# Groups of four tiles, DMA-transposed first states for all prepared tiles, and finishing work spread over two units in a five-layer graph network with GRU updates

## The reference

```
h = max(layernorm(x), 0)                          # (64, 128, 128)
A = (adj != 0)
for l in range(5):
    m   = h @ weight[l]
    agg = einsum('bij,bid->bjd', A, m)
    gi, gh = agg @ w_ih.T + b_ih, h @ w_hh.T + b_hh    # each split in r, z, n
    r, z = sigmoid(i_r + h_r), sigmoid(i_z + h_z)
    n = tanh(i_n + r * h_n)
    h = (1 - z) * n + z * h
out = x + h * nodemask[..., None]
```

## Time and profile before

| | |
|---|---|
| median of 3 runs | 381.57 us |
| the profiled execution's own time | 382.65 us |
| its span, first to last instruction | 380.9 us |
| busy: TensorE, VectorE, ScalarE, GpSimd | 96%, 82%, 78%, 73% |
| mean granted TensorE clock | 0.990 |
| share of time of the 16 DMA engines in the main queue | 52.4% |

### The profile page before, as it was taken

The page is one execution under the profiler, slowest core; times in us unless marked ns, Lnnn a source line. Parts: engine busy times, 40 slices in busy tenths (PEclk is TensorE's granted clock), DMA queues, the critical chain, the costliest instruction groups (busy, mean ns, idle before and its releaser), DMA issues.

```text
span 380.9 us, 6557 instructions
## 1 busy us (share of the span) xinstructions
PE 366.4 (96%) x2160; PEld 185.5 (49%) x2160; DVE 313.4 (82%) x574; ACT 297.1 (78%) x490; POOL 277.8 (73%) x261
## 2 busy tenths in 40 slices
PE   7769999999999999999999999999999999999992
PEld 3335555555555545445454545544455555555541
DVE  4794889888877879998989989887977778777785
ACT  3975889989878889798888978778767777677663
POOL 3555797797797889968685876757876655555796
PEclk9998999999999999999999999999999999999997
DMA  7836256387453844745285593407833432296422
GB/s 221 215 35 138 53 115 139 59 190 146 115 156 83 167 91 105 151 100 112 55 157 121 104 190 96 110 18 159 160 81 83 96 73 55 55 222 176 102 83 83
DMA packets 114128, 44.46 MB, mean 117 GB/s; under 512 B 91168, under 2 KB 107808, under 8 KB 114096
## 3 DMA queue, kind: packets, MB, share of 16 engines
q1 hardware_dynamic: 113856, 43.73, 52.4%
q10 hardware_dynamic: 144, 0.26, 0.2%
q0 software_dynamic: 96, 0.07, 0.1%
HBM read 17.57 MB, written 4.19 MB: 57 GB/s over the span
## 4 chain that ended last, share of the span: by engine, by line
PE 84%; DVE 7%; DMA 3%; POOL 2%; ACT 2%; issue 1%; SPq 0%; DVEq 0%; POOLq 0%; ACTq 0%
PE ps_r L270 9%; PE ps_r L271 8%; PE ps_z L270 8%; PE ps_r L272 8%; PE ps_z L271 8%; PE ps_z L272 8%; PE ps_s L341 4%; PE ps_s L340 4%; PE ps_in L272 4%; PE ps_in L271 4%; PE ps_in L270 4%; PE ps_hn L272 4%; PE ps_hn L270 4%; PE ps_hn L271 4%; DMA fold_in<-in_fold_lhs 1%
## 5 line engine op out<-in xcount | busy, mean ns | idle before, releaser
L747 POOL TENSOR_TENSOR zh<-z,h 128x512 f32<-128x512 f32 x80 | 101.6, 1270 | 81.3 <-ACT z L452 81.0
L446 ACT ACTIVATE r<-ps_r,b_sum,unscale 128x512 f32<-128x512 f32 x80 | 62.2, 778 | 51.1 <-PE ps_r L272 50.4
L577 DVE SCALAR_TENSOR_TENSOR rhn<-ps_hn,b_hn,r 128x512 f32<-128x512 f32 x80 | 60.0, 750 | 19.7 <-ACT r L446 19.4
L456 ACT ACTIVATE ps_in<-ps_in,b_ih,unscale 128x512 f32<-128x512 f32 x80 | 60.0, 750 | 19.0 <-DVE ps_in L583 17.2
L752 POOL TENSOR_TENSOR hp<-h,hp 128x512 f16<-128x512 f32 x64 | 74.4, 1162 | 0.0
L583 DVE TENSOR_TENSOR ps_in<-ps_in,rhn 128x512 f32<-128x512 f32 x80 | 56.0, 700 | 16.7 <-PE ps_in L272 14.6
L589 DVE SCALAR_TENSOR_TENSOR ps_in<-z,ps_in 128x512 f32<-128x512 f32 x79 | 54.6, 691 | 11.0 <-ACT ps_in L456 11.0
L452 ACT ACTIVATE z<-ps_z,b_sum,unscale 128x512 f32<-128x512 f32 x80 | 61.6, 770 | 1.0 <-PE ps_z L272 1.0
L594 DVE TENSOR_TENSOR h<-zh,ps_in 128x512 f32<-128x512 f32 x78 | 53.6, 688 | 9.7 <-POOL zh L747 1.9
L571 DVE TENSOR_TENSOR s_lo<-ps_s,s_hi 128x512 f16<-128x512 f32 x80 | 54.4, 681 | 0.0
L440 ACT CAST s_hi<-ps_s 128x512 f16<-128x512 f32 x80 | 46.6, 583 | 0.7
(11 more groups left out here) (109 smaller groups left out, 751.6 us busy)
## 6 DMA issues: line engine op xcount, KB each, us to landing
x_in<-in_x SPq DMA_DIRECT2D x16, 256.0 KB, 4.5
adj_in<-in_adj SPq DMA_DIRECT2D x16, 256.0 KB, 4.3
x_out<-in_xT SPq DMA_DIRECT2D x16, 256.0 KB, 3.0
mask_in<-in_mask_row SPq DMA_DIRECT2D x16, 256.0 KB, 3.7
out<-x_out SPq DMA_DIRECT2D x15, 256.0 KB, 2.3
nat<-hp SPq DMA_TRANSPOSE x64, 3.1
fold_in<-in_fold_lhs SPq DMA_DIRECT2D x1, 320.0 KB, 5.5
out<-x_out ACTq DMA_DIRECT2D x1, 256.0 KB, 2.6
```

The lines of the kernel that those rows point to most:

```text
L446: nc.scalar.activation(r[:], ps_r[:], ACT.Sigmoid, bias=b_sum[:, 0:1], scale=unscale[:, 0:1]).then_inc(r_done, 1)
L456: nc.scalar.activation(ps_in[K % 2][:], ps_in[K % 2][:], ACT.Tanh, bias=b_ih[:, 2:3], scale=unscale[:, 0:1]).then_inc(n_done, 1)
L577: nc.vector.scalar_tensor_tensor(out=rhn[:], in0=ps_hn[:], scalar=b_hn[:, 0:1], in1=r[:], op0=ALU.add, op1=ALU.mult).then_inc(rhn_done, 1)
L747: nc.gpsimd.tensor_tensor(zh[:, K % 2], z[:, K % 2], h[:, t % RING], ALU.mult).then_inc(zh_done, 1)
```

## The change

Groups are 4, 4, 4, 4. The planes are used for all tiles that are prepared (4 to 15), so TensorE transposes only the first states of tiles 0 to 3 (needed at the start). The join is two copies of two graphs each, in stages 8 and 9; preparation has ten stages and so begins a unit earlier relative to the tile's first layer. With these groups `prep` is 4, 7, 10, 13, 18, 23, ... 53 for tiles 4 to 15 (before: 1, 4, 7, 10, 13, 16, 21, 26, ... 46), and `ends` is 17, 20, 23, 26, 37, 40, 43, 46, 57, 60, 63, 66, 77, 78 for tiles 0 to 13 (before: 17, 20, 23, 26, 45, 48, 51, 54, 57, 60, 75 to 78). Mask and sum are in two successive units, where the next unit has no end of its own. The masked state of tile 15 is made in unit 77, not 75.

```diff
-GROUPS = (4, 6, 6)
+GROUPS = (4, 4, 4, 4)
-HALVES = 10
-FINISH = 5
-STAGES = 9
+FINISH = 3
+STAGES = 10
...
+    adds = {t: ends[t] + (ends[t] + 1 not in ending and ends[t] + 2 < N) for t in ends}
+    adding = {adds[t]: t for t in ends if t < TILES - 2}
+    storing = {adds[t] + 1: t for t in ends}
     fetching = {ends[t] - FETCH: [t] for t in ends}
-    fetching[N - FINISH - FETCH].append(TILES - 1)
+    fetching.setdefault(N - FINISH - FETCH, []).append(TILES - 1)
...
                 if K in tile_at_stage[6]:
                     transpose_first(tile_at_stage[6][K])
-                    if tile_at_stage[6][K] >= HALVES:
-                        transpose_halves(tile_at_stage[6][K])
-                if K - 1 in ending:
-                    store(ending[K - 1])
+                    transpose_halves(tile_at_stage[6][K])
+                if K in storing:
+                    store(storing[K])
...
-                if tile_at_stage[5].get(K, HALVES) < HALVES:
-                    transpose_first(tile_at_stage[5][K])
                 aggregate(K + 1)
...
-                if K in tile_at_stage[6] and tile_at_stage[6][K] < HALVES:
-                    transposed(tile_at_stage[6][K])
-                if K in tile_at_stage[6] and tile_at_stage[6][K] >= HALVES:
+                if K in tile_at_stage[6]:
                     split(tile_at_stage[6][K])
...
-            def join(t):
-                dve.wait_ge(halves_loaded[t % 2], 16 * ((t - HALVES) // 2 + 1))
+            def join(t, half):
+
+                dve.wait_ge(halves_loaded[t % 2], 16 * ((t - FIRST) // 2 + 1))
                 if t >= RING:
                     dve.wait_ge(masked, t - RING + 1)
-                nc.vector.tensor_copy(h[:, t % RING].bitcast(U16).rearrange("p (c b) -> p b c", b=2),
-                               halves_t[:, t % 2].rearrange("p (b g) c -> p b (g c)", b=2)).then_inc(h_init, 1)
+                two = slice(2 * half, 2 * half + 2)
+                state = h[:, t % RING].rearrange("p (g c) -> p g c", g=TG)[:, two].rearrange("p g c -> p (g c)")
+                joined = nc.vector.tensor_copy(state.bitcast(U16).rearrange("p (c b) -> p b c", b=2),
+                                               halves_t[:, t % 2].rearrange("p (b g) c -> p b g c", b=2)[:, :, two].rearrange(
+                                                   "p b g c -> p b (g c)"))
+                joined.then_inc(h_init if half else half_joined, 1)
...
-                if tile_at_stage[8].get(K, 0) >= HALVES:
-                    join(tile_at_stage[8][K])
+                for half in range(2):
+                    if K in tile_at_stage[8 + half]:
+                        join(tile_at_stage[8 + half][K], half)
...
+            def masked_result(t):
+                f = t % FRING
+                pool.wait_ge(ends_loaded[f], 32 * (t // FRING + 1))
+                pool.wait_ge(h_done, at[t, LAST] + 1)
+                nc.gpsimd.tensor_tensor(mask_in[:, f], mask_in[:, f], h[:, t % RING], ALU.mult).then_inc(masked, 1)
+
             def final(t):
...
                 if K in ending and K < N - 1:
-                    final(ending[K])
+                    masked_result(ending[K])
+                if K in adding:
+                    final(adding[K])
```

More of the change, by code:

```diff
@@ L157, in gnn_kernel @@
         nat_hi_init, nat_lo_init = sem("nat_hi_init"), sem("nat_lo_init")
-        split_done = sem("split_done")
+        split_done, half_joined = sem("split_done"), sem("half_joined")
         h_hi_init, h_lo_init, h_init = sem("h_hi_init"), sem("h_lo_init"), sem("h_init")
@@ L212, in transpose_halves @@
             def transpose_halves(t):
-                sp.wait_ge(split_done, t - HALVES + 1)
-                if t - HALVES >= 2:
+                sp.wait_ge(split_done, t - FIRST + 1)
+                if t - FIRST >= 2:
                     sp.wait_ge(h_init, t - 1)
@@ L405, in layernorm @@
                     act.wait_ge(nat_lo_init, t - LN + 1)
-                    act.wait_ge(t_mm, min(t - LN + 1, HALVES))
+                    act.wait_ge(t_mm, min(t - LN + 1, FIRST))
                 for q in (2 * half, 2 * half + 1):
@@ L432, in split @@
                 act.wait_ge(h0_done, 2 * t + 2)
-                if t - HALVES >= 2:
-                    act.wait_ge(halves_loaded[t % 2], 16 * ((t - HALVES) // 2))
+                if t - FIRST >= 2:
+                    act.wait_ge(halves_loaded[t % 2], 16 * ((t - FIRST) // 2))
                 nc.scalar.copy(halves[:, t % 2], h0[:, t % LN].bitcast(U16).rearrange("p (c b) -> p b c", b=2)).then_inc(
@@ L756, in final @@
                 if t < TILES - 2:
-                    pool.wait_ge(ends_loaded[f], 32 * (t // FRING + 1))
-                    pool.wait_ge(h_done, at[t, LAST] + 1)
-                    nc.gpsimd.tensor_tensor(mask_in[:, f], mask_in[:, f], h[:, t % RING], ALU.mult).then_inc(masked, 1)
                     pool.wait_ge(masked, t + 1)
```

## The result

The changed kernel takes 380.4 us (median of 22 runs, 378.97 to 381.9), the kernel before 381.16 (22 runs, 380.49 to 383.52); ratio 0.9971, 95% interval 0.9960 to 0.9983. The ratio is that of the means of the runs (the two medians are only 0.76 us apart), and by it the change gains 1.1 us (0.65 to 1.5), where 2.8 was forecast. The time lies in the stated range, 376.9 to 381.3, but the gain falls 1.7 us short of the forecast.

What follows compares the result with a forecast made beforehand. TensorE, busy 96% of the span, was taken to bound the kernel at 4.332 us a unit. Terms -2.64 - 1.93 + 0.5 + 0.7 + 0.5 + 0.1 = -2.8 us gave 378.8 us from 381.57, range 376.9 to 381.3.

Steps and rivals of the forecast that it cites:

- TensorE's transposes, -2.64: Tiles 4 to 9 by planes instead of TensorE: six units lose 0.44 us each of work on the path.
- The old stalls, -1.93: Units 25 to 55: stalls from whole joins on VectorE and from mask and sum together on GpSimd go, 1.93 us.
- Pieces, +0.5: Join pieces on VectorE ending late behind GpSimd or other instructions in listed units cost 0.5 us, bounds 0 and 5.5.
- Unit 13 and the SP queue, +0.5: Planes ahead of unit 13's state transpose in the SP queue make it land late for its reader: 0.5 us, bounds 0 and 1.4.
- ScalarE 0, bounds 0 and 0.3: ScalarE's longer copies (+0.45 us in six units) stay hidden before TensorE needs `r`, just so in units 10 and 13.
- The way back, +0.7 at units 37 and 57: State transposes of units 34 and 54, issued late in the SP queue, land 0.36 us over the margin, twice; bounds 0 and 1.6.
- margin of 2.1 us: In groups of four, a state's DMA transpose lands about 2.1 us before the aggregation that reads it.
- inside the 2.2: GpSimd, at most 1.4 us late after the change, stays within the about 2.2 us before TensorE notices.
- End, +0.1: Masked last state moved to unit 77 delays GpSimd's last sum, so the end is 0.1 us later, bounds 0 and 0.7.
- The forecast's base: The forecast of 378.8 us started from the earlier kernel's median of 381.57 us and subtracted 2.8.
- pieces over offset 5.17 in every unit: Rival: every join piece waits for a whole GpSimd instruction, ends at offset 5.40, 5.5 us on 24 pieces; 383.8 us, chance 0.08.
- The way back is late in groups of four: Rival: each of twelve prepared tiles holds a state transpose back by 0.36 us, 4.3 in all; 381.9 us, chance 0.18.

Runs made afterwards that it cites:

- moments_earlier: Changed kernel with only tile 7's moments moved on VectorE from unit 13 to 11; one execution, units 12 and 15 stall 1.29 us together, nothing gained.
- ln_later: Changed kernel with layernorm halves of tiles 5, 6 and 7 a unit later on ScalarE; one execution, stalls in units 3 to 24 1.02 us.
- preps_early: Changed kernel with preparation of tiles 4 to 7 begun in units 1, 4, 8, 13; median 378.94 us, ratio 0.9936 to the kernel before.
- fetch_shift: Changed kernel with 12 of 24 warming matmuls replaced by 48 short ones, 72 TensorE instructions more, same TensorE time; single time 382.67 us.
- ends_spread: Changed kernel with mask and sum of finished tiles moved to units 21/22, 26/27, 31/32 of each 20; median 378.24 us, ratio 0.9919 to before.

## Why the prediction was wrong in size

- *TensorE's transposes, -2.64*: right. Only 16 matmuls of line 352 are left, and units 9, 12, 18 and 21 run at the pace.
- *The old stalls, -1.93*: right, what made them is gone; units 25 and 45 stall again, but by the negation.
- *Pieces, +0.5*: the units in which a negation meets a late low half came as told, 0.52 for 0.32. The 24 pieces take 1.04 us in the mean, under the 1.3 forecast, and a quiet one costs nothing. The units called for 0.04 to 0.09 cost nothing. The overruns that the prediction lists add to 0.74 even without unit 19, not to its "0.5 to 0.9" with it; unit 19 cost nothing.
- *Unit 13 and the SP queue, +0.5, and "ScalarE 0, bounds 0 and 0.3"*: here the prediction failed most. The loss in units 14 to 17 was 1.28, and none of it came by the path that the 0.5 was for: the transpose behind the planes was in time by 0.2 us. Two other paths made it, both put at nothing. The join piece in unit 13 is not in the prediction's list of late pieces; it stood behind the moments and behind a low half just begun, and moments_earlier shows unit 14's 0.49 to be VectorE's. On ScalarE I had units 10 and 13, "together about 0.7 us late, which is just inside the time". But unit 16 has a half layernorm and a copy too and is not named; `r` is 0.9 late there, and ln_later shows 0.35 of unit 17 to be this. For the other 0.44 the cause stays open between the two engines. preps_early leaves 0.04 of the whole, but it moves hp and planes as well.
- *The way back, +0.7 at units 37 and 57*: the margin of 2.1 us was right, the place wrong, and the size 1.2. I added up lateness in the SP queue, and GpSimd's lateness (1.4 at most, "inside the 2.2") only against TensorE's need of `zh`. The low half shares that lateness (0.8 and 1.3 measured), and its own margin of 2.1 also has to pay for a transpose that lands 0.9 to 1.9 us late under an instruction transfer. The slow landing was in view, but the prediction uses it only as a bound for unit 13. The place I had named shows in fetch_shift, with 0.92, and there a transfer met the planes ahead.
- *End, +0.1*: +0.2.
- *Sum*: stalls and end were put at 1.8 and came to 3.2; -1.4 of the forecast gain. The rest of the difference to -1.1 is inside the interval.
- *The forecast's base*: the median of before was 381.57 of 3 runs and is 381.16 of 22, so the forecast of 378.8 began 0.4 too high; the gain is not touched by it. The profiled execution of before had 1.4 us in units 0 to 2 that its other profile does not have, so comparing own times of two profiles would have called the prediction exact.
- *Rivals*: pieces over offset 5.17 in every unit did not happen (a quiet piece ended 0.08 ahead of that, and this was enough). "The way back is late in groups of four" happened in part, at two units of twelve.

## What to carry to other kernels

When a kernel runs at the pace of one engine, slack is spent by the sum of what is late in a chain, not by each engine alone: write for every unit what each engine does beyond its base, and move whatever meets into free units. Here that was worth 3.2 us by the medians (2.9 in the middle) beyond the change, at no cost in work. Two profiles should be cut at the same unit before they are compared; and a deadline that a DMA has to meet needs room for its slowest landing on top of its issuer's delay.

## What the runs showed of the hardware

- A DMA transpose of a state, alone in its queue, landed in 3.0 to 3.1 us, but in 4.0 to 5.0 where a 16 KB instruction transfer of q8 began 1.0 to 2.4 us after its issue (13 of 13 in fourteen profiles). It is the same unit in both profiles of the changed kernel, and another when TensorE's program gets 72 instructions more ahead of it (fetch_shift) or the transpose is issued earlier (ends_spread).
- A VectorE copy of 512 16-bit elements takes 0.45 us where it issues ahead of GpSimd's instruction (146.17 us in the changed kernel's timeline of VectorE) and, in the same kernel, 0.9 to 1.4 where it has to wait for one; a GpSimd low half with such a copy in its first moments took 1.34 to 1.38 and not 1.15.

```profile
146.17 0.45 DVE L628 COPY h<-halves_t 128x512 uint16<-128x512 uint16 x1
```
